# Second layer's feed forward of a two-layer gated cross-attention kernel: tokens regrouped by routed expert into 17 blocks, their loads, ranks and products spread over the attention steps

## What is computed

```python
# per layer: x = x + tanh(g_xattn) * attention(layernorm(x), ctx); x = x + tanh(g_ffn) * ffn(layernorm(x))
def _L1_ffn_ref(x, gate_w, w1, b1, w2, b2, sw1, sb1, sw2, sb2):
    xf = x.reshape(-1, D)
    gate_probs = jax.nn.softmax(xf @ gate_w.T, axis=-1)
    top1 = jnp.argmax(gate_probs, axis=-1)                    # one of 2 experts
    one_hot = jax.nn.one_hot(top1, N_ROUTING, dtype=xf.dtype)
    masked = xf[None, :, :] * one_hot.T[:, :, None]           # other tokens are zeroed
    h = jax.nn.relu(jnp.einsum('end,edh->enh', masked, w1) + b1[:, None, :])
    expert_out = jnp.einsum('enh,ehd->end', h, w2) + b2[:, None, :]
    routing_output = expert_out.sum(axis=0)
    shared = jax.nn.relu(xf @ sw1 + sb1) @ sw2 + sb2
    return (routing_output + shared).reshape(B, S, D)
```

## Time and profile before

| | |
|---|---|
| median of 3 runs | 2660.89 us (2656.8 to 2661.18) |
| the profiled execution | 2655.57 us, its span 2653.8 us |
| busy, share of the span | PE 87%, PEld 73%, DVE 56%, ACT 48%, POOL 39% |
| mean granted TensorE clock | 0.958 of 2.4 GHz |
| layer 1 | from about 1359 us to the end |

### The profile page before, as it was taken

How to read it: one execution, slowest core, us unless ns; L and a number is a source line. 1 busy time by engine, 2 the same in 40 slices (tenths; PEclk the granted TensorE clock), 3 DMA queues, 4 the chain that set the end, 5 groups by cost and what they waited for, 6 DMA issues and landing times. The chain is left out here.

```text
span 2653.8 us, 48232 instructions
## 1 busy us (share of the span) xinstructions
PE 2302.0 (87%) x16128; PEld 1929.3 (73%) x16128; DVE 1493.3 (56%) x3906; ACT 1267.8 (48%) x3971; POOL 1022.9 (39%) x910
## 2 busy tenths in 40 slices
PE   5888888888888888888456999999999999999998
PEld 4667777777777777776344777877777887777777
DVE  3467667676766776767645445444444544444441
ACT  5655566555556555556023444433344443334441
POOL 1355564555554555555512333221233322123320
PEclk8999999999989999999677999999999999999999
DMA  4000000000000000000040000000000000000000
GB/s 145 14 6 17 13 16 4 16 16 16 16 12 4 16 16 16 16 4 9 4 161 1 13 17 16 16 16 16 4 12 16 16 16 16 16 4 12 16 9 9
DMA packets 25856, 51.66 MB, mean 19 GB/s; under 512 B 6272, under 2 KB 7040, under 8 KB 24640
## 3 DMA queue, kind: packets, MB, share of 16 engines
q1 hardware_dynamic: 25792, 50.84, 5.7%
HBM read 42.44 MB, written 8.39 MB: 19 GB/s over the span
## 5 line engine op out<-in xcount | busy, mean ns | idle before, releaser
L1157 POOL TENSOR_SCALAR l_probs<-l_probs,l_rinv 128x256 f32<-128x256 f32 x512 | 238.9, 482 | 587.0 <-DVE l_rinv L1372 585.3
L1268 ACT ACTIVATE l_probs<-l_score,l_negmax 128x256 f32<-128x256 f32 x512 | 238.9, 473 | 264.6 <-DVE l_negmax L1367 264.6
L335 POOL TENSOR_TENSOR l_prod<-l_att,l_kv 128x2048 f32<-128x2048 f32 x64 | 288.3, 4545 | 181.2 <-DVE l_att L608 181.2
L321 POOL TENSOR_TENSOR l_prod<-l_q,l_kv 128x2048 f32<-128x2048 f32 x64 | 290.3, 4548 | 151.7 <-DVE l_att L591 80.8
L1572 PE MATMUL l_ffn<-l_w,l_hid 128*128 128x256 f32 x1536 | 347.1, 381 | 1.0 <-ACT l_hid L1242 1.0
L1572 PEld LDWEIGHTS l_ffn<-l_w,l_hid 128*128 128x128 f32 x1536 | 287.0, 190 | 50.1 <-issue 13.5
L1379 DVE COPY l_probsT<-l_attn 128x512 f32<-128x512 f32 x256 | 175.4, 685 | 157.6 <-PE l_attn L1535 157.3
L681 DVE CUSTOM_DVE_ANT_0 l_probs<-l_score,l_mbias 128x256 f32<-128x256 f32 (+1 forms) x512 | 161.2, 352 | 140.2 <-PE l_score L877 91.8
L1367 DVE TENSOR_REDUCE l_negmax<-l_score 128x2 f32<-128x512 f32 x256 | 174.9, 683 | 64.4 <-PE l_score L1523 64.4
L614 DVE TENSOR_REDUCE l_h<-l_prod 128x128 f32<-128x2048 f32 x64 | 146.3, 2286 | 103.4 <-POOL l_prod L335 102.4
L427 ACT COPY l_probsT<-l_attn 128x384 f32<-128x384 f32 x256 | 121.1, 473 | 143.8 <-PE l_attn L887 143.8
(11 more groups left out here) (273 smaller groups left out, 7441.9 us busy)
## 6 DMA issues: line engine op xcount, KB each, us to landing
l_ctxin<-in_ctx SPq DMA_DIRECT2D x32, 256.0 KB, 3.0
l_xin<-in_x SPq DMA_DIRECT2D x16, 256.0 KB, 2.7
l_x<-in_x SPq DMA_DIRECT2D x16, 256.0 KB, 2.6
x<-l_acc SPq DMA_DIRECT2D x16, 256.0 KB, 2.0
l_xin<-x SPq DMA_DIRECT2D x16, 256.0 KB, 3.3
l_x<-x SPq DMA_DIRECT2D x16, 256.0 KB, 2.7
out<-l_x SPq DMA_DIRECT2D x16, 256.0 KB, 2.0
l_hid<-in_w SPq DMA_DIRECT2D x2, 1536.0 KB, 9.7
```

Source lines behind the costliest of these rows:

```text
L321: nc.gpsimd.tensor_tensor(prod[:, u].rearrange("p (h g d) -> p h g d", h=half, g=H), q4[:, u * half:(u + 1) * half].unsqueeze(2).to_broadc ...
L335: nc.gpsimd.tensor_tensor(prod[:, u].rearrange("p (h d g) -> p h d g", h=half, d=HD), a4.unsqueeze(2).to_broadcast([P, half, HD, H]), v4.u ...
L1157: last = nc.gpsimd.tensor_scalar(probs[:, j % 4, t * S:(t + 1) * S], probs[:, j % 4, t * S:(t + 1) * S], rinv[:, j, t:t + 1], 1.0, ALU.mul ...
L1268: last = nc.scalar.activation(probs[:, s % 4, t * S:(t + 1) * S], ps[:, t * S:(t + 1) * S], ACT.Exp, bias=negmax[:, s, t:t + 1], accum_out ...
```

## The change

- Tokens are scattered into a DRAM buffer `slots` of 17 x 256 rows: expert 0's from the front, expert 1's from the back, in order of arrival. A row (`ROW` = 260 floats) holds x3, the token's number, mean and inverse deviation. The gap between the two groups is filled with dummy rows first. 17 blocks of 256 rows then hold one expert each, whatever the routing. A dummy row's result goes to rows of `out` that the host drops.
- A block takes h0 to h3 from its expert's weights (e1), h4 to h7 from the shared ones: 96 and 32 products. What the other expert gives to each token is the constant `ce`, made once between passes 0 and 1 (`other_expert`).
- `route` (VectorE, step 4) is the gate on x3. `rank` (TensorE, step 8) counts with four small products, `place` (VectorE, step 8) makes the row numbers, `scatter` (GpSimd, after head 8) issues two indirect DMAs. `choose` picks the next block and its expert; SyncE reads both into registers and loads the block, the expert's parts (2 x 1 MB from `e1_parts`, DRAM), its biases, w2 (1 MB) and `ce`. `store` issues two indirect DMAs to `out`.
- Order: sequence a's tokens are scattered in pass a + 1; block f is loaded and transposed in pass f + 2, multiplied in pass f + 3, finished in pass f + 4. So passes 0, 1 and 2 have no feed forward, 3 to 15 have one, and four blocks (13 to 16) come after pass 15. Up products are at steps 0 to 7 and down products at 9 to 19, three a step; nothing of the feed forward follows `attn_out` any more.
- w1 is split in three pieces of 2048 columns (steps 4, 8, 14 of pass 0), where it was two of 3072; the expert parts are stored to DRAM. The third waits for the first expert's store, since it uses the same tiles.

```diff
+        ffn = Banks(nc, ctx, "l1_ffn", ["xfT"] + [f"h{j}" for j in range(8)] + ["y"])
...
+        hidden_at = {s: s for s in range(8)}
+        down_at = {9 + n: (3 * n, min(3 * n + 3, NT * 2 * NHC)) for n in range(11)}
+        split_at = {4: 3, 8: 4, 14: 5}
...
+                def load_block(d):
+                    wait_apart(sp, sp_passed, choice_ready, d + 1)
+                    e = sp.value_load(choice[0:1, 0:1], min_val=0, max_val=1)
...
+                        wait_apart(sp, sp_passed, scattered, 32 * (d + 2))
...
+                def scatter(r):
+                    wait_apart(pool, pool_passed, slot_ready, r + 1)
+                    for t in range(NT):
+                        nc.gpsimd.indirect_dma_start(slots, bass.IndirectOffsetOnAxis(slot[:, t:t + 1], 0), row[:, t], None).then_inc(scattered, 16)
...
-                def body(a, b, c, nxt):
-                    if b is not None:
-                        ffn_norm(b)
-                    if c is not None:
-                        ffn_final(c)
-                    if b is not None:
-                        low(ffn, "xfT", b, xfT, xfT_hi)
-                        low(ffn, "x0T", b, x0T, x0T_hi)
+                def body(a, r, d, f, done, nxt):
+                    if r is not None:
+                        dve.drain()
+                        variance(x3, statF, mvF, varF, varF_ready)
+                    if done is not None:
+                        ffn_final(done)
                     for s in range(STEPS):
...
+                        if r is not None and s == 4:
+                            route(r)
+                        if r is not None and s == 8:
+                            place(r)
+                        if d is not None and s == 8:
+                            choose(d)
...
+                def rank(r, f):
...
+                    pe.wait_ge(wins_ready, r + 1)
+                    T.matmul(ps[:, 0:NT], above[:], first_wins[:], start=True, stop=False)
...
-                def body(a, b, nxt):
-                    if b is not None:
-                        pe.wait_ge(xf_ready, b + 1)
-                        transpose4(ffn, "xfT", b, xf)
-                        transpose4(ffn, "x0T", b, x0)
+                def body(a, r, f, d, nxt):
...
+                        if r is not None and s == 8:
+                            rank(r, f)
+                        if f is not None:
+                            if s in hidden_at:
+                                ffn_up(f, hidden_at[s])
+                            if s == 9 and r is not None:
+                                pe.wait_ge(rank_read, r + 1)
+                            if s in down_at:
+                                ffn_down(f, *down_at[s])
+                        if d is not None and s == STEPS - 2:
+                            pe.wait_ge(xf_ready, d + 1)
+                            transpose4(ffn, "xfT", d, xf)
...
-                    if b is not None:
-                        for piece in range(4):
-                            ffn_down(b, 1, piece)
```

More of the change, by code:

```diff
@@ L36 @@
 HPC1 = P // SLOT
+ROW = D + 4
+NBLOCK = B + 1
+NSLOT = NBLOCK * S
 LN_EPS = 1e-5
@@ L1180, in body @@
                             normalise(a, j)
-                        if b is not None and j == 1:
-                            copy_residual(b)
-                        if b is not None and j == 3:
-                            other_tokens(b)
+                        if f is not None and j == 1:
+                            if not first(f):
+                                store(f - 1)
+                            copy_residual(f)
+                        if r is not None and j == 8:
+                            scatter(r)
                         if nxt is not None and j == 5:
@@ L1440, in body @@
                                 project(ahead_at[s], nxt)
-                        if first(a) and s in (4, 8):
-                            split(NS_FIRST + (s - 4) // 4)
-                    if b is not None:
-                        if not first(b):
-                            dve.wait_ge(x4_stored, 16 * b)
-                        ffn_sum(b, 0)
+                        if d is not None and s == 15:
+                            block_normalise(d)
+                        if d is not None and s == STEPS - 1:
+                            low(ffn, "xfT", d, xfT, xfT_hi)
+                        if first(a) and s in split_at:
+                            split(split_at[s])
                     if a is not None:
@@ new lines, in ffn_down @@
+                def ffn_down(f, lo, hi):
+                    ps, full, free, turn = ffn.at("y", f)
+                    if lo == 0:
+                        pe.wait_ge(free, turn)
+                        pe.wait_ge(e2_in, 32 * (f + 1))
+                        ffn.emptied(pe, "h7", f)
+                    for n in range(lo, hi):
+                        t, c = n // (2 * NHC), n % (2 * NHC)
+                        w = e2[:, c, :] if c < NHC else w2[:, c - NHC, :]
+                        last = T.matmul(ps[:, t * D:(t + 1) * D], hid[:, c, t * P:(t + 1) * P], w, start=c == 0, stop=c == 2 * NHC - 1)
+                    if hi == NT * 2 * NHC:
+                        last.then_inc(full, 1)
@@ L1576, in project, with other_expert @@
+                def other_expert():
+                    ps = ffn.bank[0]
+                    pe.wait_ge(relu_ready, 1)
+                    pe.wait_ge(e2_raw_in, 32)
+                    for e in range(2):
+                        for c in range(NHC):
+                            last = T.matmul(ps[:, e * D:(e + 1) * D], hid[:, e * NHC + c, 0:P], (e2, w2)[e][:, c, :], start=c == 0, stop=c == NHC - 1)
+                    last.then_inc(other_full, 1)
                 def project(use, a):
```

383 lines of the change are left out of this document (261 added, 122 removed).

## The result

| | before | after |
|---|---|---|
| median of the runs, us | 2659.95 (4 runs) | 2690.61 (4 runs, 2684.64 to 2700.57) |
| profiled execution, us; its span | 2655.6; 2653.8 | 2684.64; 2682.8 |
| mean granted clock of TensorE | 0.958 | 0.927 |

The changed kernel takes 1.0119 of the time before, 95% interval 1.0104 to 1.0134. It is slower by 1.2%, where 2617 us and a gain of 1.6% were forecast; 2690 also lies above the range, which ended at 2672.

What follows compares the result with a forecast made beforehand. TensorE's products were taken to bound the kernel. A mixed pass was 77.3 - 15.8 + 7.6 = 69.1 us; start +4.5, passes -109.2 and tail +61.4 gave -43.3, so 2617 us; range 2555 to 2672.

Steps and rivals of the forecast that it cites:

- the clock's: TensorE's granted clock in mixed passes: 0.96, 2.0 us lost in 13 passes and 4 for the others, +30 us.
- rival (b): Waits pull TensorE's clock down two or three times a pass: 4 us more in 13 passes, 2669 us; chance 0.08.
- Products: TensorE in mixed passes: products and transposes removed, rank added, old waits filled or gone; -15.8 us a pass.
- Boundary wait: At the pass boundary, TensorE waits 3.3 us before step 2's scores, for VectorE's chain and head 1's exponential.
- Gate, rank: Step 4: route delays head 5's exponential, about 2.85 us; step 9: down products wait 1.4 us for the rank's read.
- GpSimd and DMAs: Indirect DMAs take 1.3 us of GpSimd each, hidden up to 3.6; weight loads of 8 to 11 us hidden too.
- rival (c): An indirect DMA holds GpSimd longer than 3.6 us; at 5 us each the time is 2690 us; chance 0.07.
- Start: Pass 0: third split waits for the first expert's store, +3 us (0 to 39); with slow clock, +4.5.
- Rival (d): Dummy rows and stores at 150 GB/s hold the third split back: 36 us more, 2653 us; chance 0.10.
- Passes 1, 2 and tail: Attention-only passes of 54.8 and 56.5 us, other_expert +12.5 between passes 0 and 1; 116.3 us after the last attention.
- Rival (a): Waits overlap more and the clock stays up: 2538 to 2590 us, middle 2564; chance 0.25.

Runs made afterwards that it cites:

- e1_fill: Changed kernel with TensorE's three waits filled by products whose result is thrown away (26, 30 and 12 a pass): 2623.5 us, 0.9864 of the kernel before.
- e2_final_early: Changed kernel with VectorE's addition of the feed forward's output moved from the next pass's start to its own pass's end: 2632.8 us, 0.9916 of the kernel before.
- e5_all_waits: Changed kernel with addition at its own pass's end, gate in three parts, first down piece last in step 9, variance later: 2531.0 us, 0.9524 of before.
- e10_rank_wait: e5_all_waits with the first down product and its wait for the rank ahead of step 9's other products again: 2565.9 us, 0.9666 of the kernel before.
- e7_gap_late: e5_all_waits with the fill of the slots issued after the stores of expert 2's low parts, from its own tile: 2527.6 us, 0.9499 of the kernel before.
- e8_fill_start: Changed kernel with only the wait before a pass's first hidden product filled, by 26 unused products: 2682.1 us, 1.0088 of the kernel before.

## Why the prediction was wrong

The sum for the profiled execution was 2612.3 us; it took 2684.6, 72.3 more. By the starts of line 1549, which the trace gives as 1451.34, 1522.12, 1581.59, ... 2488.28, 2559.40:

| stretch | forecast | measured | miss |
|---|---|---|---|
| start, first end of attention | 1447.5 | 1451.3 | +3.9 |
| pass 1 with `other_expert` | 67.3 | 70.8 | +3.5 |
| pass 2 | 56.5 | 59.5 | +3.0 |
| 12 mixed passes | 827.6 + 24 for the clock | 906.7 | +55.1 |
| the last mixed pass | 65.4 + 2 | 71.1 | +3.7 |
| tail | 116.3 | 123.4 | +7.1 |
| clock of the other passes, in the rows above now | 4 | | -4.0 |

**The step that failed** is the clock's: 2.0 us for each mixed pass, and as its end "at 0.96 it loses at most 0.04 x 69.1 = 2.8 us". The 0.96 was read off layer 0 by the share that TensorE is busy there, 88%, and carried over to a pass as busy but with other gaps. The pass was as busy as forecast (65.49 of 75.3 us, 87%) and the clock 0.93, and the price is 5.2 us by e1_fill. The busy share doesn't give the clock: in the changed kernel's own trace layer 0 is busy for 505.54 of 586 us, 86%, at 0.98, with no idle time of over 2.2 us, and a mixed pass for 87% at 0.93, with two, of 3.3 and 3.7 us. 13 x 3.2 = 42 of the 72 us are this term.

The forecast had the case as rival (b), waits that pull the clock down two or three times a pass, deciding from a granted clock of about 0.92, with a chance of 0.08. Its mechanism is what happened, three times a pass, at 0.92 to 0.93. Its price of 6 us (4 more than 2.0) is near the 5.2 measured, and its 2669 us is still 21 short, for the other misses of the table; its place in the chances was wrong, and the earlier trace rows had shown it: a gap-ridden 3 us followed by 3.4 us at 0.51. Three waits were forecast, with nearly their lengths; that each of them would be such a stretch wasn't put together.

**Products.** Right: 64 records of down products and 96 of hidden units in a pass, for 96 and 144, and the products' prices as they were. The pass without clock loss is 70.65 us by e1_fill against 69.1 in the sum.

**Boundary wait.** Its size was forecast at 3.3 and is 3.31, but at another place and for another reason: not before the scores of step 2 for an exponential, but before the first hidden product, which shares its bank with the sum that `ffn_final` reads. That the two sizes agree is chance. The chain on VectorE up to `ffn_final` was right. That two things end at nearly the same time is shown by e2_final_early: with the addition gone, 1.45 us of the forecast's own wait remain.

**Gate, rank.** 2.85 forecast and 3.7 measured; 1.4 and 1.7. The waits together are 8.7 for 7.6 us. With the boundary's they are in three different places of the pass, as said, and none hid another.

**GpSimd and DMAs.** An indirect DMA holds GpSimd for 0.98 us (1.3 forecast, 3.6 needed to matter), so rival (c) has fallen; that its time for 5 us a DMA, 2690, is the one measured is chance. All of one line in the changed kernel, in ns, shortest, median, longest:

```profile
L1252 POOL DMA_INDIRECT slots<-l_row,l_slot x32: 958/976/1236, 1496.3 to 2578.7; - x32
```

The rule cited from the Trainium skill (SBUF — State Buffer, "SBUF: two separate sides"), that such a DMA stalls while VectorE holds the ports, can't be seen here: shortest and longest of the 32 are 0.28 us apart, and whether VectorE held the ports at those times isn't recorded. The loads of the weights were hidden: from 1700 to 2300 us no engine waits for a DMA in the changed kernel or in e5_all_waits, which moves 76 GB/s.

**Start.** The third split waited 9.2 us for its store where 3 had been taken. ScalarE arrives 25.9 us after the fill is issued (26 forecast), but the store lets it go on only after 35.0, where 23 to 33 had been given. The sum had the bytes and not SyncE's wait of 12.9 us for the fill. Rival (d) had a late store too, by a slow transfer and with 36 us more; the whole start is late by 3.9 only.

**Passes 1, 2 and tail.** Each is long by 3 to 7 us. In passes 1 and 2 TensorE has waits of 2.9 to 3.9 us too, and the granted clock is 0.85 and 0.89 in the windows 1450 to 1520 and 1520 to 1600. In the tail TensorE waits 3.9 us for `ffn_final` at its start, and the granted clock is 0.97; no experiment took it apart further. The tail's own parts (29.5 + 27.5 + 26.9 + 26.3 + 7) give some 117 and not the 116.3 that the sum used.

**Rival (a)**, waits that overlap and a clock that stays up, 2564 us, didn't come. It describes what the order can reach once the waits are gone: 2531.

Open: what decides whether a given wait is followed by a short, a long or no stretch at the lower clock. The runs show only that it varies for the same wait, between passes of one execution, and that a pass without any wait of over 1.2 us can have such a stretch too.

## What to carry to other kernels

Before taking products off the engine that bounds a kernel, list what those products covered, and move the covered chains (here the last addition, the gate, the read of the rank) to places where other products still run: the same change was 1.2% slower with three bare waits and 4.8% faster without them. When you sum up the new order, price an idle time of TensorE of a few us in a dense stretch at its length and the slower clock behind it (here 5.2 us on waits of 8.7), and don't read the clock off the busy share. A cheap test that tells the clock from the wait is to fill the wait with products that nobody reads: if the pass gets shorter, it was the clock. Fill all the waits for that: one alone gave 0.8 of the 5.2 us.

## What the runs showed of the hardware

- The three idle times of a pass of the changed kernel (3.3, 3.7 and 1.7 us) have a stretch at the lower level of the clock behind them in each of the eleven full mixed passes. With 1.7 us as the only one of over 1.2 it was so in 3 of 9 passes (e10_rank_wait), and with none of over 1.2 in 3 of 9 as well (e7_gap_late) or in none (e5_all_waits). The Trainium skill (TensorE: Matmul & The Clock Gate, "HAM oscillation — how this bites in real kernels") warns of idle gaps from a certain length on; two of the three waits here are shorter than that, and the clock fell behind them too. Where the two differ, the trace decides.
- A kernel with one such wait a pass has executions of two lengths, 2554 and 2576 us, on one chip, of the same program, with 0.01 between their mean granted clocks.
- Taking away one of several waits can lengthen the slow stretch behind another (3.4 in most passes to 6.8 us in all, in e8_fill_start), so that filling the first wait of a pass gained 0.8 us where 1.7 to 2.3 were expected.
- Two transfers of 2210 KB, issued one behind the other, landed 12.7 and 18.9 us after their issue. SyncE waited 12.9 us for them before it could issue what follows, a store of 1 MB among it, and by that ScalarE waited 9 us and TensorE 11.
